# Loading W2's natural copy in one burst instead of one piece a tile, in a graph attention and feed-forward kernel

## The reference, cut to what matters

```python
def gat_layer(x, W, att_src, att_dst, bias, src, dst, heads, out_ch):
    h = (x @ W.T).reshape(n, heads, out_ch)
    a_src = jnp.einsum('nhc,hc->nh', h, att_src)
    a_dst = jnp.einsum('nhc,hc->nh', h, att_dst)
    e = leaky_relu(a_src[src] + a_dst[dst], 0.2)
    alpha = softmax of e over the edges that end in one node
    return segment_sum(alpha * h[src], dst) + bias

h   = relu(gat_layer(layernorm(x), W1, ..., heads=8, out_ch=128))
x   = x + gat_layer(h, W2, ..., heads=1, out_ch=768)
x   = x + ffn(layernorm(x))      # 6 class rows by routed experts, the rest fc1, gelu, fc2
```

## Time and profile before

| what | value |
|---|---|
| median of 3 runs | 700.55 us (698.9 to 701.09) |
| the profiled execution's own time | 700.23 us |
| its span in the trace | 698.4 us |
| PE busy (matmuls) | 686.0 us, 98% |
| DVE, ACT, POOL busy | 511.5 us, 441.1 us, 125.2 us |
| DMA moved | 88.37 MB |

### The profile page before, as it was taken

One profiled execution on the slowest core, in us unless ns is written; L12 is line 12 of the kernel. 1 busy time (PEld: TensorE's weight loads), 2 busy tenths in 40 slices (PEclk: granted clock), 3 DMA queues, 4 the chain that ended last, 5 costly groups with the idle time before them and its releaser, 6 DMA issues.

```text
span 698.4 us, 13751 instructions
## 1 busy us (share of the span) xinstructions
PE 686.0 (98%) x4757; PEld 645.6 (92%) x4757; DVE 511.5 (73%) x866; ACT 441.1 (63%) x900; POOL 125.2 (18%) x150
## 2 busy tenths in 40 slices
PE   7999999999999999999999999999999999999997
PEld 6799999789999999999999899999998999999997
DVE  7888875999899999999998754434668643837232
ACT  6666766388999999999999744454261434422202
POOL 2224130001121202121121000000243330333302
PEclk9999999999999999999999999999999999999999
DMA  8737998868434334334323231101973544315102
GB/s 278 240 95 220 253 260 224 212 194 280 77 78 85 93 56 106 70 78 90 61 22 74 73 111 60 59 1 49 303 224 115 161 133 161 99 59 187 34 23 69
DMA packets 54430, 88.37 MB, mean 127 GB/s; under 512 B 17763, under 2 KB 37081, under 8 KB 54378
## 3 DMA queue, kind: packets, MB, share of 16 engines
q1 hardware_dynamic: 43798, 65.69, 32.8%
q0 software_dynamic: 6080, 8.17, 7.4%
q10 hardware_dynamic: 4500, 13.82, 6.0%
HBM read 68.09 MB, written 15.33 MB: 119 GB/s over the span
## 4 chain that ended last, share of the span: by engine, by line
PE 86%; DVE 5%; DMA 4%; ACT 3%; issue 1%; ACTq 1%; DVEq 0%; POOL 0%; SPq 0%
PE bank L1490 19%; PE bank L1630 13%; PE bank L1451 12%; PE bank L1554 12%; PE bank L1347 9%; PE bank L1734 4%; DMA w1n_sb<-in_W 3%; PE bank L1706 3%; PE bank L1264 2%; PE bank L1608 2%; PE bank L1760 1%; DVE x2f L2386 1%; PE bank L1496 1%; PE bank L1497 1%; ACT w_hi L1050 1%
## 5 line engine op out<-in xcount | busy, mean ns | idle before, releaser
L1490 PE MATMUL bank<-PT,h1s 125*128 125x250 f32 x660 | 147.6, 374 | 0.0
L1490 PEld LDWEIGHTS bank<-PT,h1s 125*128 125x128 f32 x660 | 121.3, 190 | 13.5
L2151 DVE SCALAR_TENSOR_TENSOR L<-asb,nad 125x1250 f32<-125x1250 f32 x80 | 120.8, 1546 | 1.2 <-PE bank L1451 0.7
L2162 DVE CUSTOM_DVE_ANT_0 L<-L,LC 125x1250 f32<-125x1250 f32 x80 | 114.2, 1459 | 1.3
L965 ACT ACTIVATE L<-L,nm 125x1250 f32<-125x1250 f32 x80 | 109.7, 1373 | 6.1 <-DVE nm L2162 4.8
L1451 PE MATMUL bank<-ident,L 125*125 125x125 f32 x800 | 94.0, 273 | 0.0
L1451 PEld LDWEIGHTS bank<-ident,L 125*125 125x125 f32 x800 | 91.1, 189 | 0.8 <-issue 0.4
L986 ACT COPY PT<-bank 125x500 f32<-125x500 f32 x165 | 83.8, 618 | 2.7 <-PE bank L1451 2.7
L778 POOL DMA_DIRECT2D PT_diff<-PT x34 | 28.4, 837 | 157.8 <-ACT PT L986 157.8
L1962 DVE TENSOR_TENSOR hot<-iota,edges 125x750 f16<-125x750 f16 x100 | 46.9, 540 | 7.6 <-PE bank L1264 5.4
L1630 PE MATMUL bank<-h_hi,PT_hi 125*125 125x384 f32 x200 | 41.5, 350 | 0.0
(11 more groups left out here) (289 smaller groups left out, 1341.3 us busy)
## 6 DMA issues: line engine op xcount, KB each, us to landing
asb<-src_logit_rows SPq DMA_DIRECT2D x14, 416.5 KB, 3.5
atom_w<-in_atom_inT SPq DMA_DIRECT2D x5, 1152.0 KB, 13.5
atom_w<-in_atom_outT SPq DMA_DIRECT2D x5, 1152.0 KB, 9.7
log_count_scratch<-LCw SPq DMA_DIRECT2D x10, 546.9 KB
LC<-log_count_scratch SPq DMA_DIRECT2D x10, 546.9 KB
LCt<-log_count_scratch SPq DMA_DIRECT2D x10, 546.9 KB
h_scratch<-h1st ACTq DMA_DIRECT2D x10, 448.0 KB
PT_diff<-PT POOLq DMA_DIRECT2D x34, 122.1 KB, 3.0
```

Of the source, the lines that this page charges most:

```text
L1490: mm = pe.matmul(sums, h1s[q][:, s, :], PT[p][:, s, :], start=(s == (0 if plain else PART + 2)), stop=(plain and s == NT - 1))
L2151: dve.scalar_tensor_tensor(L[s % RING][:, :], asb[q][0:NP, 1, :], nad1[:, ds(h, 1), t:t + 1].rearrange("p h t -> p (h t)"), asb[q][0:NP, 0 ...
L2162: dve.tensor_tensor_reduce(out=L[s % RING][:, :], in0=L[s % RING][:, :], in1=LC[:, t, :], scale=-1.0, scalar=-FLOOR, op0=ALU.add, op1=ALU.min,
```

## The change

SP now waits for `wattp` right behind its load of tile 3 of x, issues all six loads of W2's natural copy one after the other, and only then begins with the stores and loads of the logarithms. In the loop nothing is left but these. The same DMAs with the same sizes and semaphores are issued; two kinds of them change places in SP's queue.

```diff
@@ -505,14 +505,13 @@
             sp.wait_ge(sq_ready, 1)
             load_x(3)
+            sp.wait_ge(wattp, 1)
+            for k in range(KD):
+                load_w2n(k)
             store_lc(0)
             for i in range(1, 8):
                 store_lc(i)
                 load_lc(i - 1)
-                if i == 1:
-                    sp.wait_ge(wattp, 1)
-                else:
-                    load_w2n(i - 2)
```

## The result

| | before | after |
|---|---|---|
| median, lowest to highest of 22 runs each | 699.68 us (698.49 to 703.09) | 702.59 us (700.75 to 707.68) |
| ratio of the times | | 1.0042 [1.0029, 1.0056] |
| profiled execution, its span | 700.23 us, 698.4 us | 703.94 us, 702.0 us |

The change made the kernel slower by 0.42%, about 2.9 us. The forecast was 700.1 us and no change that can be told, with a range of 698.8 to 702.1 us; the result lies outside it.

A forecast was written before the change was run, and what follows sets the result against it. PE, busy 98% of the span, was taken as the bound, only its idle time recoverable. All terms were 0 except -0.5 us at 62 us: 700.55 - 0.5 = 700.1 us, no change that can be told, range 698.8 to 702.1.

The forecast's parts named there:

- The burst: Six W2 loads issued together from 31.4 us, 3.15 MB landing by 44.5 to 47 us; cost taken as 0.
- The second rival: Burst stays queued until about 50 us, ACT's issues there held 4.0 us; +0.9 us, 701.4 us in all; chance 0.12.
- The gain at 62 us: ACT's held store issues shorten without W2's first load beside them, easing PE's wait before 68.14 us; 0.5 us gained.
- the first rival: The hold of ACT's issues at 62 us was never W2's, so nothing is gained; 700.5 us; chance 0.25.
- The two signs named for this place: ACT's two issues at 62 us in under 3.1 us; PE's wait before 68.14 us under 0.5 us.
- Six loads are taken out between 64 and 118 us: Step on the loop: 3.15 MB, 22% of that stretch's traffic, and six SP issues go; 0.5 us gained.
- The one place where PE pays for a full DMA side is the 0.87 us: PE's 0.87 us wait before 68.14 us, behind ACT's 4.01 us hold at 61.83, claimed as the only such cost.
- below, 0: Lower bound of the gain from removing the load beside ACT's issues at 62 us; the upper was 1.10 us for PE.
- the row at 61.83: ACT's two issues of `store_h1` at 61.83 us, held 4.01 us, the worst of their kind in the trace.
- The POOL rival: POOL misses DVE's idle gap near 77 us, its small L717 slows, 4.7 us lost, 705.3 us; chance 0.05.

The follow-up runs named there:

- e11: Changed kernel with 32 empty PE instructions and SP's stores of logarithms of tiles 2 and 5 waiting for ACT's stores of tiles 2 and 4; 701.11 us.
- e14: e5 plus an SP wait that keeps its store of logarithms of tile 2 behind ACT's store of tile 2; 700.29 us, ratio 1.0 to before.
- e7: Changed kernel, SP waiting for ACT's stores before its read-back of tile 1 and its store of logarithms of tile 5; 700.38 us, ratio 1.0012 to before.
- e5: Changed kernel with only the third load (k = 2) back in its old place in the loop; 699.44 us, ratio 1.0004 to before.
- e1: Changed kernel, unaltered, run again for a second profile; 702.21 us, ratio 1.0029 to before.
- e3: Kernel before with all six W2 loads out of the loop, issued together behind tile 7's read-back near 124 us; 706.87 us, ratio 1.0096.
- e15: Kernel before plus only the SP wait that keeps its store of logarithms of tile 2 behind ACT's store of tile 2; 701.53 us.
- e8: Changed kernel with SP instead of ACT storing the products of tiles 0 to 7, each store placed where its data is ready; 701.39 us.
- e2: Changed kernel with the six loads also issued again in their old places in the loop; 699.91 us, ratio 1.0005 to before.
- e16: e5 with the third load issued by ACT instead of SP; 700.56 us, ratio 1.0009 to before.
- e17: e5 with the third load issued by POOL instead of SP; 700.52 us, ratio 1.0006 to before.
- e18: Changed kernel with four loads early, k = 2 and 3 in the loop at i = 4, and e14's SP wait; 699.78 us, ratio 0.9996 to before.
- e9: Changed kernel with 32 empty PE instructions ahead of the products with W1; 703.27 us, ratio 1.0038 to before.
- e10: Kernel before with 32 empty PE instructions ahead of the products with W1; 700.04 us, ratio 0.9996.

## Why the prediction was wrong

- **The burst** (wait, six issues, bytes, who is in flight with it): right. It was issued from 31.34 to 35.87 us (forecast 31.4 to 35, or up to 44), the six issues took 4.53 us inside the bounds of 2.1 and 12.3, store 0 began at 44.46, and PE's only wait there, 0.16 us at 43.21, stood in before too (0.15).
- **The second rival**, that the burst doesn't drain: did not occur; the share of 0.85 at 295 GB/s until 45 us is the 3.85 MB that were reckoned, though a share of 0.9 or more had been forecast. A slip without effect: slices 4 to 8 end at 140 us, not 158.
- **The gain at 62 us**, forecast 0.5 us: mis-sized. ACT's pair took 3.85 us instead of 4.01 with no load of W2 beside it, and PE's wait went from 0.87 to 0.69. So the first rival was right at that place: the hold was never W2's. The prediction read the overlap of two issues as a cause; e11 and e14, beside e7, show that the store of logarithms ahead is one (0.92 and 0.80 us once SP waits). The two signs named for this place, under 3.1 us and under 0.5 us, both failed.
- **The step that failed** is "Six loads are taken out between 64 and 118 us", with its sentences "The one place where PE pays for a full DMA side is the 0.87 us" and, for the bounds, "below, 0". It took for granted that removing a transfer can only relieve. ACT's issues at 87.27, 0.79 + 0.84 us with no cover behind them, were not priced, since nothing was held there in before. With the third load ahead of them they were mostly free (before, e5), without it mostly held (after, e1, e3). The range was bounded by the idle time that could be recovered, and not by the issues that could become dear: a hold like that of the row at 61.83 at this place is 4.01 - 0.84 = 3.2 us, all of it PE's; the profiled execution gave 2.4, and 1.5 us for the clock on top. That row stood in the prediction, and it was used for 39 and 50 us only.
- **The clock.** "The prediction is wrong if PE's idle time before 137 us changes by more than 1.1 us, or if PE's matmuls change in length": both happened. The idle time in front of the sixth tile is 2.4 us more, and 18 matmuls at 1.2 GHz cost 1.46 us on top.
- **The POOL rival** did not occur: L716 took 1.83 us at 76.80, as before.
- **The Trainium skill** (DMA: Bandwidth & Descriptors, section Queues, rings and completion order) says that each DMA engine takes turns, packet by packet, between the queue rows that have work. The prediction worked out from it, beside its forecast, that ACT's issues would not be held by SP's transfers and the gain at 62 us would be nothing. The gain was indeed near nothing (0.2 us of PE's wait), but ACT's issue was held all the same: 0.81 to 0.92 us with SP's store kept back (e7, e11), 2.4 to 3.9 us behind it. The rule is about packets, and no run here shows their turns; what it was taken to say of issues, the runs contradict.

**What stays open:** by what means the third load keeps ACT's issues free, why its removal alone costs only 1.0 of the 2.9 us, why x's issue is held when SP issues nothing, and why e15 and e8 cost more than their rows show.

## What to carry to other kernels

A transfer that nobody waits for can still change how often the DMA issues of another queue are held, so before one is moved, list the DMA issues of every in-order engine behind it, with the cover that each has, and price each at the longest issue of its kind in the trace: where the cover is thin, the lower bound of a removal is not 0. Where the time of a kernel has two kinds of runs, one profile can fall on either (e2, e16, e17); count the runs beside it before a mechanism is built on its rows.

## What the runs showed of the hardware

- Two pairs of DMA issues on ACT took 0.78 + 0.80 us in e18 and 2.42 + 1.62 us in e1 for the same bytes, and ACT computed nothing while they lasted. The profile books it as "issue", with no releaser.
- With SP's store of logarithms issued ahead, ACT's pair at 62 us took 2.91 to 4.18 us, and with the store kept back 0.80 to 0.92 us (e11, e14, e15, e18).
- More traffic made the kernel no slower: e2 moves 3.15 MB twice in 699.91 us; e1, beside it, moves it once in 702.21.
- PE's clock fell to 1.2 GHz after pauses of 2.0 to 2.6 us in seven of the profiled executions (4.5 to 4.6 us for 18 matmuls of 3.1), and not in two, after 2.55 us (e1) and 2.15 us (e2). Of after's 22 runs, 13 have a mean clock below 1.00 and a median of 703.94 us, nine have 1.00 and 702.14. What decides it was not found.
- Empty PE instructions (32 in e9 and e10) do not appear in the page's instruction count (13750 in after and in e9), and the time did not change beyond noise (e10's ratio is 0.9996).
